# Eight heads at once: wide softmax stages, logarithm-and-Newton inverse lengths and two-bank evacuations in a two-attention kernel

## The chip, the cores and the metric

One core of one Trainium2 chip runs the kernel; all arithmetic is fp32 (two masks are bf16). The metric is the device time of one execution in microseconds. Before the change three runs gave 1178.49 to 1179.34 us, median 1179.04 us.

## The reference, cut to what matters

Eight sequences of 512 rows and 128 features go through a first attention (16 query heads on 8 key heads, causal, full length), a residual and a layer norm. Then come two layers of a windowed attention with a gated feed-forward, and a last layer norm.

```python
def _layer(x, wqkv, qs, ksc, wo, lg, lb, w1, b1, w2, b2):   # twice
    q, k, v = split(shift_token(x) @ wqkv)     # 8 heads of 64
    q = l2norm(q) * qs; k = l2norm(k) * ksc    # each head to length 1
    q, k = rotary_xpos(q, k)
    o = local_attention(q, k, v)               # windows of 64 see themselves and the one before,
    x = x + o @ wo                             # softmax over 128 keys, scores times 8
    h = (layer norm of shift_token(x)) * lg + lb
    a, g = split(h @ w1 + b1); h = a * gelu(g)
    return x + h @ w2 + b2
```

## The kernel before

The rows are cut into 32 tiles of 128. The first attention (steps whose names begin with a_) goes tile by tile through 8 batches of 4 tiles; a tile's keys grow from 128 to 512. The second attention (b_ steps) handles one tile of one layer at a time; such a pair is called a place here, and there are 64. A layer-1 place follows its layer-0 place by a group or two of two tiles, and the last two tiles are groups of their own. The feed-forward runs by groups.

**Order.** No queue is left to chance. `make_plan` lists every step with its engine, a cost in ns, the steps it needs, and the PSUM banks that it fills and who empties them. `in_order` simulates the five engines from these costs, the handover times `LAG` and `MARGIN` and the priorities `HURRY`, and writes out a fixed order for each engine and a bank for each PE step. Every engine then walks its list and waits on semaphore counts. PE's steps have a shape of the array (`HALF`, `TURN`, `COLS`, `QUARTER`); a change of shape has a price in the plan. Where PE has a planned gap over `IDLE` it gets `warm` fillers, products of the identity that nobody reads.

**One place of the second attention.** PE turns the tile (`b_h`, two banks), ACT and DVE copy it out, and PE makes q, k and v (`b_q`, `b_k`, `b_v`). ACT squares q and k (L901, L907). DVE multiplies them with two rotary tables (L1062, L1065) and POOL adds the halves (L1249). DVE sums the squares by head, for q (L1113, L1115) and k (L1120, L1122) apart, each with a floor; POOL raises both to the power -0.5 (L1262 for q, L1266 for k) and scales k (L1272). q stays unscaled. PE transposes q and k by halves of the partitions into two banks (L758); ACT copies out one bank (L922) and DVE the other (L1095). PE makes the scores of 8 heads in two banks (L776). DVE, for one head at a time, multiplies the scores with q's inverse length (keys carry a minus sign), adds the mask, writes to `b_prob` and keeps the minimum (L1107, eight a place). ACT, one head at a time, takes the exponential with that as bias and adds up the row (L930, eight a place). DVE takes the reciprocal (L1127), and POOL (L1279; ACT, L939, in the last three places) scales the probabilities. PE transposes them into two banks (L791), which ACT (L946) and DVE (L1133) copy out; then come the products with v (L807, copied to `o_t` by ACT, L952) and `wo`, a DMA shift by one row, the layer norm and the feed-forward (gelu L970, gate L1168 on DVE).

`b_prob`, `rnorm` and `r1` are two deep, PSUM has 8 banks. ACT's exponential and gelu lie in different table sets, and the loads (ACT_TABLE_LOAD) are put in by the compiler. All matrix steps of one bank go through the helper at L623 or lines of their own.

## Time and profile before

| what | before |
|---|---|
| median of 3 runs | 1179.04 us (1178.49 to 1179.34) |
| span of the profiled execution | 1177.7 us |
| what lies around that span, against the median | 1.4 us |
| busy: PE, DVE, ACT, POOL | 1151.3, 1047.6, 1010.3, 958.5 us |
| weight loads of PE | 827.0 us |
| granted TensorE clock, mean | 1.000 |
| instructions | 45569 |

The span runs from the first to the last instruction on the core. No time of the profiled execution other than its span is given. Busy time of an engine is the time in which at least one of its instructions ran; a busy PE can still be a PE whose matmuls wait for one another. PEld is the loading of weights, which goes on beside the matmuls. The shares are means over the whole kernel, whose middle repeats batch by batch and whose end has no first attention left to run.

### The profile page before, as it was taken

What the parts mean: (1) busy time and instruction counts of PE and PEld (TensorE: products, weight loads), DVE (VectorE), ACT (ScalarE), POOL (GpSimd) and SP (SyncE); (2) the same over time, 40 slices, a digit from 0 to 9 for tenths busy, and PEclk for the clock granted to TensorE, in tenths of its full rate; (3) what the DMA queues carried; (4) which work ended last, traced back from release to release, by engine and by line L of the source; (5) the groups of instructions that cost most, each with busy time, mean ns of one, the idle gap of its engine ahead of it and who ended that gap; (6) DMA issues with size and microseconds to landing.
All of it is one profiled execution on the core that took longest, in us unless ns stands there. A gap on an engine that the chain in (4) does not pass through costs nothing.

```text
span 1177.7 us, 45569 instructions
## 1 busy us (share of the span) xinstructions
PE 1151.3 (98%) x17652; PEld 827.0 (70%) x17652; DVE 1047.6 (89%) x4019; ACT 1010.3 (86%) x3168; POOL 958.5 (81%) x950
## 2 busy tenths in 40 slices
PE   9999999999999999999999999999999999999997
PEld 7667766767667667677676776777766767666666
DVE  6888998989999999989989899898998989999883
ACT  6888889897988989899898988889799887987784
POOL 2777878889878897888888888888987889888772
PEclk9999999999999999999999999999999999999999
DMA  6000010100011010100100101001101100010110
GB/s 228 19 13 22 16 30 22 27 14 22 21 27 27 14 31 12 31 23 22 31 17 18 27 19 31 16 18 28 26 13 26 27 13 23 12 31 19 24 27 13
DMA packets 31095, 31.87 MB, mean 27 GB/s; under 512 B 12576, under 2 KB 21408, under 8 KB 30752
## 3 DMA queue, kind: packets, MB, share of 16 engines
q1 hardware_dynamic: 30448, 28.17, 9.2%
q8 instruction: 141, 2.31, 0.8%
q10 hardware_dynamic: 432, 0.79, 0.2%
q14 instruction: 74, 0.61, 0.2%
HBM read 10.07 MB, written 2.10 MB: 10 GB/s over the span
## 4 chain that ended last, share of the span: by engine, by line
PE 78%; ACT 12%; DVE 5%; issue 2%; POOL 1%; DMA 1%; SPq 0%; POOLq 0%; DVEq 0%; ACTq 0%
PE psum L623 36%; PE psum L662 11%; PE psum L698 11%; PE psum L675 6%; PE psum L776 5%; PE psum L807 4%; ACT b_prob L930 3%; PE psum L791 3%; PE psum L758 2%; ACT prob L874 2%; ACT L930 2%; ACT L970 1%; ACT u_t L970 1%; ACT b_prob_t L946 1%; DVE x L1190 1%
## 5 line engine op out<-in xcount | busy, mean ns | idle before, releaser
L874 ACT ACTIVATE prob<-prob,negmax 128x512 f32<-128x512 f32 (+3 forms) x512 | 283.4, 558 | 9.6 <-DVE negmax L1025 9.2
L1025 DVE CUSTOM_DVE_ANT_0 prob<-psum,causal 128x512 f32<-128x512 f32 (+3 forms) x512 | 228.3, 484 | 7.0 <-PE psum L662 6.5
L1229 POOL TENSOR_SCALAR prob<-prob,rowinv 128x384 f32<-128x384 f32 (+1 forms) x256 | 161.2, 644 | 58.9 <-DVE rowinv L1031 58.4
L930 ACT ACTIVATE b_prob<-b_prob,b_negmax 128x128 f32<-128x128 f32 x512 | 198.9, 394 | 0.5 <-DVE b_negmax L1107 0.2
L623 PE MATMUL psum<-wqkv,h_t 128*64 128x512 f32 x768 | 191.5, 595 | 0.7 <-ACT h_t L894 0.5
L662 PE MATMUL psum<-k_t,q_t 64*128 64x384 f32 (+3 forms) x1024 | 179.5, 452 | 5.7 <-ACT b_prob_t L946 1.8
L1249 POOL TENSOR_TENSOR r<-r 128x512 f32<-128x512 f32 x120 | 152.7, 1277 | 10.8 <-DVE r L1065 10.5
L698 PE MATMUL psum<-prob_t,v 128*64 128x256 f32 x1280 | 152.3, 379 | 0.1
L1107 DVE CUSTOM_DVE_ANT_0 b_prob<-psum,band,rnorm 128x128 f32<-128x128 f32 x512 | 146.0, 347 | 6.9 <-PE psum L776 5.6
L1279 POOL TENSOR_TENSOR b_prob<-b_prob,b_rowinv 128x1024 f32<-128x1024 f32 x61 | 116.2, 1905 | 39.3 <-DVE b_rowinv L1127 39.3
L698 PEld LDWEIGHTS psum<-prob_t,v 128*64 128x64 f32 x1280 | 91.4, 137 | 59.0 <-issue 23.7
L1037 DVE COPY prob_t<-psum 128x512 f32<-128x512 f32 (+1 forms) x176 | 112.2, 638 | 7.4 <-PE psum L675 4.4
L675 PEld LDWEIGHTS psum<-ident,prob 64*128 64x128 f32 x2560 | 98.3, 139 | 26.2 <-issue 21.6
L1266 POOL TENSOR_TENSOR rnorm<-length,minus_half 128x8 f32<-128x8 f32 x64 | 106.0, 1656 | 9.4 <-DVE length L1122 9.3
L1232 POOL TENSOR_TENSOR prob<-prob,rowinv 128x512 f32<-128x512 f32 x96 | 99.2, 1053 | 15.9 <-DVE rowinv L1031 15.9
L675 PE MATMUL psum<-ident,prob 64*128 64x64 f32 x2560 | 111.1, 224 | 1.0 <-ACT b_prob_t L946 0.2
L1262 POOL TENSOR_TENSOR rnorm<-length,minus_half 128x8 f32<-128x8 f32 x64 | 106.3, 1661 | 4.5 <-DVE length L1115 4.5
L881 ACT COPY prob_t<-psum 128x512 f32<-128x512 f32 (+1 forms) x176 | 96.4, 548 | 13.5 <-PE psum L675 12.0
L874 ACT ACTIVATION_READ_ACCUMULATOR prob<-prob,negmax 128x1 f32 x512 | 98.8, 193 | 0.0
L930 ACT ACTIVATION_READ_ACCUMULATOR b_prob<-b_prob,b_negmax 128x1 f32 x512 | 98.3, 192 | 0.0
L623 PE MATMUL psum<-f_t,w 128*64 128x256 f32 (+1 forms) x816 | 91.4, 370 | 0.4 <-ACT f_t L961 0.3
L1062 DVE TENSOR_TENSOR r<-psum,table 128x512 f32<-128x512 f32 x128 | 86.6, 677 | 2.5 <-PE psum L623 1.1
(104 smaller groups left out, 2739.8 us busy)
## 6 DMA issues: line engine op xcount, KB each, us to landing
vb_mid<-vb SPq DMA_DIRECT2D x112, 128.0 KB, 2.3
x_t<-in_x_t SPq DMA_DIRECT2D x8, 256.0 KB, 3.1
x_n<-in_x SPq DMA_DIRECT2D x8, 256.0 KB, 2.9
x<-x SPq DMA_DIRECT2D x64, 31.8 KB
out<-x SPq DMA_DIRECT2D x15, 128.0 KB, 2.3
wqkv<-in_wqkv SPq DMA_DIRECT2D x1, 1536.0 KB, 11.3
w<-in_w SPq DMA_DIRECT2D x1, 768.0 KB, 13.4
x<-x SPq DMA_DIRECT2D x48, 0.2 KB
```

The costliest lines, as they stand in the source:

```text
L623: last = mm(out[half(w)], weights[:, half(w)], moving, start=start, stop=stop)
L662: last = mm(banks[h][:, p * K:(p + 1) * K], q_t[half(h), (NT * b + i) % 2, c + p, :], k_t[half(h), b % 2, (c + p) // 2, 0:K], start=True, ...
L675: last = transpose(banks[q][:, o:o + E], prob[half(q), k % PROBS, h, j * P:(j + 1) * P], ident[half(q), half(q)])
L698: last = mm(bank[half(h), p * P:(p + 2) * P], v[:, (NT * b + j) % V_RING, g * E:(g + 1) * E], two_pairs(k % PROB_TS, np_, i, h, p, j), sta ...
L874: last = af(pr, pr, ACT.Exp, bias=negmax[:, k % 4, o:o + 1], scale=-1.0, accum_out=rowsum[:, k % 4, o:o + 1])
L930: last = af(pr, pr, ACT.Exp, bias=b_negmax[:, a, o:o + 1], scale=-1.0, accum_out=b_rowsum[:, a, o:o + 1])
L1025: vec.tensor_tensor_reduce(prob[:, k % PROBS, h, p * K:(p + 1) * K], bank[:, p * K:(p + 1) * K], causal[:, S - K:S], -E ** -0.5, 3.0e38, A ...
L1037: vec.tensor_copy(prob_t[:, k % PROB_TS, 1, 0:n], bank[:, 0:n]).then_inc(prob_t_dve, 1)
L1107: vec.tensor_tensor_reduce(b_prob[:, a, s, c, :], bank[:, c * P:(c + 1) * P], band[:, min(n % NT, 2 - n % 2), :], rnorm[:, a, 0, 2 * c + s ...
L1229: last = gp.tensor_scalar(pr, pr, rowinv[:, k % 4, h:h + 1], 1.0, ALU.mult, ALU.mult)
L1249: return gp.tensor_tensor(r1[:, a, s, :, :], r1[:, a, s, :, :], r2[:, s, :, :], ALU.add)
L1279: gp.tensor_tensor(pr, pr, b_rowinv[:, a, :].unsqueeze(2).broadcast_to([P, HB, P]), ALU.mult).then_inc(b_prob_ready, 1)
```

## The change

The diff rewrites the second attention's side work and leaves PE's matmuls as they are.

- **Softmax in one operation a stage.** DVE adds the mask to the scores of all 8 heads out of both banks (`b_mask`), and takes the maxima of all heads in one reduction (`b_max`). POOL subtracts them (new step `b_less`). ACT takes one exponential over 1024 columns, with no bias and no accumulator. DVE adds up the rows in one reduction ahead of the reciprocal (`b_inverse`).
- **Inverse lengths.** DVE reduces the squares of q and k together and floors them (`b_length`). ACT makes a first guess as exp(-0.5 ln(65536 length)) (`b_guess`), DVE improves it by one Newton step of three small operations (`b_root`), and POOL scales both q and k (`b_unit`) before the transposition. The two powers on POOL go. The rotary table carries the factor LIFT, and the minus sign of the keys goes.
- **Evacuations over two banks.** Where a step fills two banks (`BESIDE`), the planner now gives it neighbours. ACT alone copies out the transposed q/k and probabilities, 1024 columns at once, save in the last 8 places (`SPLIT`), where ACT and DVE still share them. The copies of h and of the normed tile take both banks in one instruction.
- **Tables.** One set that holds exponential and logarithm is used for all exponentials, and the loads are written out.
- **The plan.** Costs, `HURRY` and two constants of `in_order` are new, so the orders of all engines are, too.

```diff
+LIFT = 65536.0
+TABLE_OF = {"exp": "natural_log_exp_and_others", "gelu": "gelu_and_others"}
 BANKS, LATE = 8, 15
-SINGLES, BY_ACT, BY_DVE = 2, 3, 8
+SINGLES, BY_ACT, BY_DVE, SPLIT = 2, 3, 8, 8
...
+def takers_of(l, n):
+
+    return ("act", "dve") if PLACE.get((l, n), -1) >= len(SEQUENCE) - SPLIT else ("act",)
+def wide_ns(taker, l, n):
+    return copy_ns(taker, 512) if len(takers_of(l, n)) == 2 else copy_ns(taker, 1024)
...
+SWITCH, TABLES, SHY, PULL = {"64x128": 155, "128x64": 150, "64x64": 97}, 1283, 381, 0.041587
+HURRY = {("act", "a_exp"): -50, ("act", "a_k"): 27100, ("act", "a_q"): 750, ("act", "a_turn"): 69350,
...
+BESIDE = ("b_h", "b_turn_qk", "b_scores", "b_turn_p", "b_turn_f")
...
+        step("dve", "b_length", k, 1400, [("act", "b_square_q", k), ("act", "b_square_k", k), before and ("dve", "b_root", before)])
+        step("act", "b_guess", k, 520, [("dve", "b_length", k), before and ("dve", "b_root", before)], "exp")
+        step("dve", "b_root", k, 750, [("act", "b_guess", k), before_2 and ("pool", "b_unit", before_2)])
...
+        step("pool", "b_unit", k, 1950, [("dve", "b_root", k), ("pool", "b_rotated_k", k), (summer(*k), "b_rotated_q", k)])
...
+        step("pe", "b_scores", k, 937, [(taker, "b_turn_qk", k) for taker in takers_of(l, n)], QUARTER, [[("dve", "b_mask", k)]] * 2)
+        step("dve", "b_mask", k, 1220, [("pe", "b_scores", k), ("dve", "tables", (LAYERS - 1,)), before_2 and ("pe", "b_turn_p", before_2)])
+        step("dve", "b_max", k, 1210, [("dve", "b_mask", k)])
+        step("pool", "b_less", k, 1900, [("dve", "b_max", k)])
+        step("act", "b_exp", k, 1040, [("pool", "b_less", k)], "exp")
+        step("dve", "b_inverse", k, 1400, [("act", "b_exp", k)])
+        step(scaler(*k), "b_scale", k, 1900 if scaler(*k) == "pool" else 3100, [("dve", "b_inverse", k)])
...
+                    if s.name in BESIDE:
+                        start = max(start, min(max(bank_free[x], bank_free[x + 1]) for x in range(0, BANKS, 2)))
+                    elif s.frees:
...
+            if s.name in BESIDE:
+                _, one = min((max(bank_free[x], bank_free[x + 1]), x) for x in range(0, BANKS, 2))
+                banks = [one, one + 1]
+            else:
+                clear = [x for x in range(BANKS) if bank_free[x] <= start]
+                banks = sorted(clear, key=lambda x: ((x ^ 1) in clear, bank_free[x], x))[:len(s.frees)]
...
+        def both_banks(name, *args):
+
+            one, two = BANK_OF[name, args]
+            return psum[:, one:two + 1, :]
...
+            nc.scalar.preload_act_table_set(TABLE_OF["exp"])
+
+            def table(name):
+
+                if function[0] != name:
+                    nc.scalar.preload_act_table_set(TABLE_OF[name])
+                    function[0] = name
...
+                rows = h_t[0:E, l, t * P:(t + 1) * P].rearrange("p (q n) -> p q n", q=2)
+                copy(rows, both_banks("b_h", l, n)[0:E, :, 0:E]).then_inc(h_act, 1)
...
+            def guess_lengths(l, n):
+                act.wait_ge(length_ready, nth("dve", "b_length", (l, n)))
+                act.wait_ge(rnorm_ready, nth("dve", "b_root", before(l, n)))
+                table("exp")
+                af(guess[:], length[:], ACT.Ln, scale=LIFT).then_inc(logged, 1)
+                act.wait_ge(logged, nth("act", "b_guess", (l, n)))
+                af(guess[:], guess[:], ACT.Exp, scale=-0.5).then_inc(guess_ready, 1)
...
+                if len(takers_of(l, n)) == 2:
+                    bank, _ = banks_of("b_turn_qk", l, n)
+                    copy(qk_t[:, l, :, :, k0:k0 + E].rearrange("p s c n -> p (s c) n"), bank.rearrange("p (k n) -> p k n", k=2 * CB)).then_inc(qk_act, 1)
+                else:
+                    act.wait_ge(cleared, 1)
+                    rows = qk_t[:, l, :, :, k0:k0 + P].rearrange("p s c (q n) -> p q (s c) n", q=2)
+                    copy(rows, both_banks("b_turn_qk", l, n).rearrange("p q (k n) -> p q k n", k=2 * CB)).then_inc(qk_act, 1)
+
+            def exponentials_b(l, n):
                 a = PLACE[l, n] % 2
-                for c in range(CB):
-                    act.wait_ge(b_max_ready, CB * (nth("dve", "b_max", (l, n, s)) - 1) + c + 1)
-                    pr = b_prob[:, a, s, c, :]
-                    o = s * CB + c
-                    last = af(pr, pr, ACT.Exp, bias=b_negmax[:, a, o:o + 1], scale=-1.0, accum_out=b_rowsum[:, a, o:o + 1])
-                last.then_inc(b_exp_done, 1)
+                act.wait_ge(b_less_ready, nth("pool", "b_less", (l, n)))
+                table("exp")
+                pr = b_prob[:, a, :, :, :].rearrange("p s c n -> p (s c n)")
+                af(pr, pr, ACT.Exp).then_inc(b_exp_done, 1)
...
-            def maxima_b(l, n, s):
+            def mask_b(l, n):
                 a = PLACE[l, n] % 2
                 dve.wait_ge(late_in, 16 * 7)
                 dve.wait_ge(tables_ready, LAYERS)
                 dve.wait_ge(b_scored, nth("pe", "b_scores", (l, n)))
                 dve.wait_ge(p_turned, nth("pe", "b_turn_p", before(l, n, 2)))
-                dve.wait_ge(rnorm_q, nth("pool", "b_inverse_q", (l, n)))
-                bank = banks_of("b_scores", l, n)[s]
-                for c in range(CB):
-                    o = s * CB + c
-                    vec.tensor_tensor_reduce(b_prob[:, a, s, c, :], bank[:, c * P:(c + 1) * P], band[:, min(n % NT, 2 - n % 2), :],
-                                             rnorm[:, a, 0, 2 * c + s:2 * c + s + 1], 3.0e38, ALU.add, ALU.min, b_negmax[:, a, o:o + 1]).then_inc(b_max_ready, 1)
-
-            def length_of_q(l, n):
...
-                dve.wait_ge(rnorm_q, nth("pool", "b_inverse_q", before(l, n)))
-                vec.tensor_reduce(ssq[:, 0, :, 0], sq[:, 0, :, :], AX.X, ALU.add).then_inc(summed_q, 1)
-                dve.wait_ge(summed_q, nth("dve", "b_length_q", (l, n)))
-                vec.tensor_reduce(length[:, 0, :], ssq[:, 0, :, :], AX.X, ALU.max).then_inc(length_q, 1)
-
-            def length_of_k(l, n):
                 dve.wait_ge(sq_k, nth("act", "b_square_k", (l, n)))
-                dve.wait_ge(rnorm_k, nth("pool", "b_inverse_k", before(l, n)))
-                vec.tensor_reduce(ssq[:, 1, :, 0], sq[:, 1, :, :], AX.X, ALU.add).then_inc(summed_k, 1)
-                dve.wait_ge(summed_k, nth("dve", "b_length_k", (l, n)))
-                vec.tensor_reduce(length[:, 1, :], ssq[:, 1, :, :], AX.X, ALU.max).then_inc(length_k, 1)
+                vec.tensor_reduce(ssq[:], sq[:], AX.X, ALU.add).then_inc(summed, 1)
+                dve.wait_ge(summed, nth("dve", "b_length", (l, n)))
+                vec.tensor_scalar(length[:], ssq[:], FLOOR, None, ALU.max).then_inc(length_ready, 1)
+
+            def roots(l, n):
+                a = PLACE[l, n] % 2
+                dve.wait_ge(guess_ready, nth("act", "b_guess", (l, n)))
+                dve.wait_ge(unit_ready, nth("pool", "b_unit", before(l, n, 2)))
+                link(vec.scalar_tensor_tensor(out=shortfall[:, 0], in0=guess[:], scalar=-0.5 * LIFT, in1=guess[:], op0=ALU.mult, op1=ALU.mult))
+                link(vec.tensor_tensor(shortfall[:, 1], length[:], shortfall[:, 0], ALU.mult))
+                vec.scalar_tensor_tensor(out=rnorm[:, a], in0=shortfall[:, 1], scalar=1.5, in1=guess[:], op0=ALU.add, op1=ALU.mult).then_inc(rnorm_ready, 1)
 
             def inverse_b(l, n):
                 a = PLACE[l, n] % 2
-                dve.wait_ge(b_exp_done, nth("act", "b_exp", (l, n, 1)))
+                dve.wait_ge(b_exp_done, nth("act", "b_exp", (l, n)))
+                vec.tensor_reduce(b_rowsum[:, a, :], b_prob[:, a, :, :, :].rearrange("p s c n -> p (s c) n"), AX.X, ALU.add).then_inc(b_summed, 1)
...
-            def inverse_length_of_q(l, n):
-                pool.wait_ge(length_q, nth("dve", "b_length_q", (l, n)))
-                pool.wait_ge(b_exp_done, nth("act", "b_exp", (*before(l, n, 2), 1)))
-                gp.tensor_tensor(rnorm[:, PLACE[l, n] % 2, 0, :], length[:, 0, :], minus_half[:], ALU.pow).then_inc(rnorm_q, 1)
-
-            def inverse_length_of_k(l, n):
-                pool.wait_ge(length_k, nth("dve", "b_length_k", (l, n)))
-                gp.tensor_tensor(rnorm[:, PLACE[l, n] % 2, 1, :], length[:, 1, :], minus_half[:], ALU.pow).then_inc(rnorm_k, 1)
-
-            def unit_k(l, n):
+            def unit(l, n):
                 a = PLACE[l, n] % 2
-                pool.wait_ge(rnorm_k, nth("pool", "b_inverse_k", (l, n)))
+                pool.wait_ge(rnorm_ready, nth("dve", "b_root", (l, n)))
                 pool.wait_ge(rotated_k, nth("pool", "b_rotated_k", (l, n)))
-                gp.tensor_tensor(r1[:, a, 1, :, :], r1[:, a, 1, :, :], rnorm[:, a, 1, :].unsqueeze(2).broadcast_to([P, HB, E]),
-                                 ALU.mult).then_inc(unit_ready, 1)
+                if summer(l, n) == "pool":
+                    pool.wait_ge(rotated_q, nth("pool", "b_rotated_q", (l, n)))
+                else:
+                    pool.wait_ge(rotated_q_dve, nth("dve", "b_rotated_q", (l, n)))
+                x = r1[:, a, :, :, :].rearrange("p s h e -> p (s h) e")
+                scale = rnorm[:, a, :, :].rearrange("p s h -> p (s h)").unsqueeze(2).broadcast_to([P, 2 * HB, E])
+                gp.tensor_tensor(x, x, scale, ALU.mult).then_inc(unit_ready, 1)
+
+            def less_maximum(l, n):
+                a = PLACE[l, n] % 2
+                pool.wait_ge(b_max_ready, nth("dve", "b_max", (l, n)))
+                pr = b_prob[:, a, :, :, :].rearrange("p s c n -> p (s c) n")
+                gp.tensor_tensor(pr, pr, b_maximum[:, a, :].unsqueeze(2).broadcast_to([P, HB, P]), ALU.subtract).then_inc(b_less_ready, 1)
...
-    for s, f in enumerate((scale * np.float32(8.0), np.float32(-1.0) / scale)):
+    for s, f in enumerate((scale * np.float32(8.0 * LIFT ** 0.5), np.float32(LIFT ** 0.5) / scale)):
...
```

## Rows read from the trace of the kernel before

**Rows 1.** Page, section 1: busy us, share of the span, instructions.
```profile
PE 1151.3 (98%) x17652; PEld 827.0 (70%) x17652; DVE 1047.6 (89%) x4019; ACT 1010.3 (86%) x3168; POOL 958.5 (81%) x950
```

**Rows 2.** Chain of waits, whole span: start us, us, what, pieces.
```profile
507.67 5.22 PE psum L623 x84
...
648.94 5.23 PE psum L623 x84
```

**Rows 3.** Windows: length, busy us (instructions) by engine, clock, DMA share, GB/s.
```profile
470.60:611.90 141.30, 139.89 (x2166) 100.53 (x2164) 129.07 (x499) 125.19 (x393) 121.39 (x120) 1.00 0.09 23
...
1035.80:1117.00 81.20, 77.38 (x1236) 53.60 (x1234) 74.15 (x262) 62.87 (x185) 65.19 (x58) 1.00 0.10 24
1117.00:1131.00 14.00, 13.49 (x225) 10.05 (x220) 12.37 (x53) 13.77 (x47) 7.79 (x8) 1.00 0.05 13
1131.00:1143.00 12.00, 10.58 (x186) 7.68 (x184) 11.63 (x40) 9.78 (x36) 10.54 (x10) 1.00 0.20 48
1143.00:1157.00 14.00, 11.44 (x210) 9.26 (x212) 5.65 (x30) 12.74 (x44) 3.67 (x4) 1.00 0.03 6
1157.00:1177.70 20.70, 15.03 (x262) 12.84 (x256) 9.38 (x36) 5.10 (x13) 7.95 (x11) 0.99 0.06 17
```

**Rows 4.** Groups by line, PE: the fillers.
```profile
L623 PE MATMUL psum<-ident 128*64 128x128 f32 x284 | 19.1, 276 | 0.0
```

**Rows 5.** Waits of PE's weight loads: us in total, times, longest us.
```profile
PEld psum L623 <- ACT o_t L952: 9.5, 16, 0.7
PEld psum L776 <- ACT qk_t L922: 5.8, 8, 0.9
PEld psum L623 <- DVE u_t L1168: 4.2, 12, 0.7
```

**Rows 6.** Timeline, 1143 to 1157 us: start us, us, engine, line, op, operands.
```profile
1146.11 0.34 DVE L1107 CUSTOM_DVE_ANT_0 b_prob<-psum,band,rnorm 128x128 f32<-128x128 f32 x1
...
1146.37 0.35 DVE L1107 CUSTOM_DVE_ANT_0 b_prob<-psum,band,rnorm 128x128 f32<-128x128 f32 x1
...
1152.06 0.20 DVE L1127 RECIPROCAL b_rowinv<-b_rowsum 128x8 f32<-128x8 f32 x1 [3.10 <-ACT b_prob L930]
...
1154.18 2.43 ACT L939 ACTIVATE b_prob<-b_prob,b_rowinv 128x128 f32<-128x128 f32 x8
```

**Rows 7.** Groups by line: length sum (DVE), power and scalings (POOL).
```profile
L1279 POOL TENSOR_TENSOR b_prob<-b_prob,b_rowinv 128x1024 f32<-128x1024 f32 x61 | 116.2, 1905 | 39.3 <-DVE b_rowinv L1127 39.3
...
L1266 POOL TENSOR_TENSOR rnorm<-length,minus_half 128x8 f32<-128x8 f32 x64 | 106.0, 1656 | 9.4 <-DVE length L1122 9.3
...
L1272 POOL TENSOR_TENSOR r<-r,rnorm 128x512 f32<-128x512 f32 x64 | 67.2, 1050 | 2.7
...
L1120 DVE TENSOR_REDUCE ssq<-sq 128x8 f32<-128x512 f32 x64 | 43.6, 682 | 2.9 <-ACT sq L907 2.1
```

**Rows 8.** Groups by line: DVE tensor_tensor out of PSUM, two widths.
```profile
L1062 DVE TENSOR_TENSOR r<-psum,table 128x512 f32<-128x512 f32 x128 | 86.6, 677 | 2.5 <-PE psum L623 1.1 <-ACT sq L901 0.7
...
L1144 DVE TENSOR_TENSOR x<-psum,x 128x128 f32<-128x128 f32 x64 | 18.3, 286 | 4.4 <-PE psum L623 4.3
```

**Rows 9.** Groups by line: evacuations by DVE and ACT.
```profile
L1095 DVE COPY qk_t<-psum 128x512 f32<-128x512 f32 x64 | 43.8, 684 | 0.3 <-PE psum L758 0.2
...
L922 ACT COPY qk_t<-psum 128x512 f32<-128x512 f32 x64 | 37.3, 583 | 17.4 <-PE psum L758 17.3
...
L894 ACT COPY h_t<-psum 64x64 f32<-64x64 f32 x128 | 20.0, 207 | 7.0 <-PE psum L721 7.0
```

**Rows 10.** Chain of waits, 1085 us to the end: table load, then exponentials.
```profile
1117.97 1.28 ACT L930
1119.27 3.19 ACT b_prob L930 x16
...
1123.26 1.54 ACT b_prob L930 x8
```

154 lines of the change are left out of this document (74 added, 80 removed), and 6 rows, old and new, of the table HURRY.

## Prediction

> **What bounds the kernel now.** I read the page's busy shares first. TensorE (PE) has 1151.3 of 1177.7 us, VectorE (DVE) 1047.6, ScalarE (ACT) 1010.3 and GpSimd (POOL) 958.5 [rows 1]. PE is the bound by share, but three others are close behind, so I then asked where PE isn't busy, and who ended that. The chain of waits shows that the middle of the kernel repeats: its 5.2 us projection piece comes back every 141.3 us, four times between 366 and 796 us, of which two rows stand there (507.67 and 648.94 us) [rows 2]. That is one batch: 4 tiles of the first attention and 8 places (tile and layer) of the second. The windows of that length (five from 188.0 to 894.5 us agree to 1 us, one stands there) say that of 141.30 us PE is busy 139.9, DVE 129.1, ACT 125.2 and POOL 121.4 [rows 3]. So in the middle PE idles 1.4 us a batch, some 10 us over the seven batches that look like this. The end is another stage: from 1035.8 us on PE idles 3.8 + 0.5 + 1.4 + 2.6 + 5.7 = 14.0 us [rows 3], and most of the 19.1 us of identity products into no result (fillers that keep PE going) [rows 4] lie there, too. About 30 us at the end is thus latency, not PE work. The clock is 1.00 throughout [rows 3], so clock plays no part.
>
> PE's own waits name mostly ACT as the releaser: its o_t 9.5 and its qk_t 5.8 us of weight-load idle, against 4.2 us for u_t, the largest of DVE's [rows 5]. An ACT queue that is served late is what PE sees most.
>
> **The change, part by part, per place (64 places).** PE's matmuls are the same in number and kind, so nothing is taken from or added to its work. What changes is how loaded the other engines are, how long the chain is, and PE's order, which the planner makes anew.
>
> *DVE.* Removed: eight masked maxima at a pitch of 0.26 us [rows 6], 2.08 us; two length reductions of 0.68 [rows 7] with a small floor operation each, which I put at the reciprocal's 0.2 [rows 6], 1.76 us. The reciprocal itself stays. Added: a masked copy of 1024 columns out of PSUM. A tensor_tensor from PSUM takes 286 ns for 128 columns and 677 for 512 [rows 8], 1.02 ns a column, so 1.20 us for 1024. A reduction of 512 columns takes 0.68, so one of 1024 about 1.20 by the same slope; there are three (maximum, row sum, squares), 3.60 us. The floor and three 16-column operations of the Newton step at 0.2 each, 0.8. Five waits of DVE on its own results, no row of their own, at about 0.05 each, 0.25. Added 5.85, removed 3.84: +2.0 us a place, +128 us in all. Back come the evacuations that ACT takes over whole in 56 of 64 places: 112 x 0.684 [rows 9] = -77 us, and one instead of two small copies of h, some -10 us at the reciprocal's 0.2. Net +41 us: DVE goes from 1047.6 to about 1089 us, and in a batch from 129.1 to 134.2 of 141.3 (95%). Bounds from the rows: +30 (no own waits, Newton operations at 0.15) to +60 (masked copy at the maxima's 0.26 us per 128 columns, 2.08, and no gain at h).
>
> *ACT.* Removed: eight exponentials, 3.19 with their accumulator reads [rows 10] (0.40 each). Added: one of 1024 columns without accumulation. A copy of 64 columns takes 207 ns, one of 512 583 [rows 9], 0.84 ns a column, so 1.01 us. Two 16-column functions (logarithm, exponential) at 0.2 to 0.3 each, 0.5. Two evacuations of 1024 columns in place of 512, +0.43 each in 7 of 8 places, 0.75. Net -0.93 us a place at face value; I take -0.86, for what of the two small functions is waiting, -55 us in all: 1010 to about 955.
>
> *POOL.* Removed: the two powers, 1.66 each, and the scaling of k, 1.050 [rows 7]. Added: scaling of q and k and the subtraction of the maximum, both 128x1024 with a broadcast as the probabilities' scaling has it, 1.905 each [rows 7]. Net -0.56 us a place, -36 us: 958 to about 923.
>
> *Table loads.* The logarithm now wants its set, which is made the one for all exponentials, so a load is still needed only between gelu and an exponential. A load shows as 1.28 us, and on the chain of the end the next function starts 1.30 us after the load began [rows 10]. The new logarithm can fall into a stretch of gelus and cost two loads more; if one place in eight does, 16 loads, 21 us of ACT, which its 55 us cover. The Trainium skill (ScalarE: Activation LUTs, What ACT_TABLE_LOAD costs) gives 1283 ns plus a drain of about 1380 ns for each switch. By that page's 2.66 us the same 16 loads would be an estimated 43 us, and ACT's relief would be all but gone. The trace shows the 1283 ns but not the drain, and I stay with the row.
>
> *The chain of one place* grows. Softmax, from scores to probabilities ready to be scaled: before 0.26 + 3.19 + 0.2 = 3.7 us if nothing interferes (ACT follows DVE head by head), after 1.20 + 1.20 + 1.91 + 1.01 + 1.40 plus five handovers of 0.1 = 7.2 us: +3.5. Lengths: before, k's reduction and floor 0.9, power 1.66 and scaling 1.05 (q's power is beside it), 3.6 us; after 1.37 + 0.5 + 0.6 + 1.91 + 0.4 = 4.8: +1.2, and it must wait for q's squares too. In the middle this is covered: the next places' work and the first attention's fill PE, each place of a layer has a period of 17.7 us, and the buffers are two deep. There the price is zero unless an engine saturates. If the cover fails, it is 4.7 us for each place in series.
>
> *PSUM banks.* Scores' second bank is now released after 1.2 instead of 2.1 us, both banks of a transposition after 1.0 instead of 0.6 to 0.7, and the two must be neighbours. These about cancel; zero, between -3 and +5 us.
>
> **The sum.** Middle: PE idles 1.4 us a batch, and the queue that mostly ends those waits loses 6.9 us a batch. I take 1.0 us of the 1.4 away: 7 x -1.0 = -7 us (bounds: -10, all of it, and +15, below). Start: nothing.
>
> End: three stages of the chain [rows 10]. From 1117 to 1131 it lies on ACT, 13.77 of 14.00 us busy [rows 3], and 6.3 us of it are exponentials of two places (3.19 and 1.54 [rows 10], and two more pieces of the same line, 1.6 together), which become 2.0: -4. From 1131 to 1143 it lies on DVE, 11.63 of 12.00 busy [rows 3], which gets one to two places' worth of +2.0: +3. From 1143 on one last place is alone: its softmax runs from 1146.11 to 1152.26 [rows 6], 6.15 us, and would take 7.2, but ACT's gelu and table load held its scaling back to 1154.18 anyway [rows 6]: 0. The last length step is 1 to 3 us longer: +2. Sum +1 us (bounds -6 and +10). What is late next there is DVE.
>
> Forecast: -7 + 1 = -6 us. The profiled span is 1177.7 us and the median of the three runs 1179.04, so 1.4 us lie around the span; I keep them. 1179.0 - 6 = 1173.0 us.
>
> The skill's page Trainium Kernel Development and Optimization (Performance Expectations) says that matmul busy time tells little of how near the bound PE is, and that the weight loads' busy share tells more. Here they differ, 98% against 70% [rows 1], so more than 1.4 us a batch may be hidden in PE's busy share. By that rule a new order could give more than my -7, and it is the reason for a lower end below the sum's.
>
> **Rivals.** *DVE takes PE's place.* At 134.2 of 141.3 us DVE has 7.1 us left a batch, where it has 12.2 now. Its order is fixed ahead, so a late operand idles it. For: it would be as full as the fullest engine, and every place needs it five times in series. Against: DVE waits little for others now (its largest waits are off PE's path), and PE's waits name ACT rather than DVE [rows 5]. It decides when DVE needs more than 7 us of idle a batch. If it needs 9 of today's 12.2, a batch is 134.2 + 9 = 143.2, +1.9 us, times 8 = +15, with the end's +1: 1195; if it needs 8, +0.9 a batch: 1187. About 1190. Chance 0.25.
>
> *The longer chain sets the end.* Two places (layer 0's last tile, then layer 1's) follow in series there. If ACT's relief doesn't come on that path, each pays up to 4.7: +8 to +9, and with no gain in the middle 1188, with the middle's gain 1181. Chance 0.12.
>
> *Nothing moves.* PE's 139.9 busy us a batch remain, and the 1.4 us aren't ACT's doing but shape changes and jitter. Then the middle gives 0, the end +-1, 1179. Chance 0.15.
>
> *The planner fills much better.* Forty microseconds less work on the three side engines together let it drop fillers and changes of PE's shape; all 10 us of the middle and 6 us of the end: 1163. I count it with the forecast. Chance of forecast and this together 0.48.
>
> **How the numbers follow.** One per mille is 1.2 us; about 0.2% (2.4 us) is what a measurement of this kernel can tell from no change. Faster by more (below 1176.7) is the forecast, 0.48. Within 0.2% is the third rival, 0.15, of which its jitter gives nothing away: 0.15. Slower (above 1181.4): 0.25 + 0.12 = 0.37. Both signs are likely, so the range goes over both: down to 1160, the forecast's best case with 3 us for the unseen, up to 1192, which takes most of the DVE rival. The forecast's own range is 1162 to 1176.
>
> **What the profile after would show.** Right: a period under 140.5 us, PE idle under 0.8 us a batch, ACT near 955, DVE near 1089, POOL near 923 us. DVE rival: DVE above 95% of the middle windows, PE waits that name DVE's b_prob, b_rowinv or rnorm, a period above 142. Chain rival: the middle as forecast, but more fillers and PE idle after 1035 us. Wrong outright would be table loads that take far more of ACT than 80 us, or DVE's new operations costing over 7 us a place.

## The result and the profile after

The change makes the kernel slower: 1292.37 us median of four runs (1288.91 to 1293.72) against 1179.18 us for the kernel before on the same chip, a ratio of 1.0958 with a 95% interval of 1.0942 to 1.0975. The profiled execution took 1293.54 us, its span is 1291.7 us, and the mean granted clock 0.992. I had forecast 1173.0 us and a range up to 1192.

Page of after, section 1 (busy us, share, instructions), against [rows 1]:

```profile
PE 1208.3 (94%) x17988; PEld 850.8 (66%) x17988; DVE 1134.3 (88%) x3074; ACT 944.8 (73%) x2236; POOL 929.9 (72%) x886
```

Groups by line of after, PE: the fillers, against [rows 4].

```profile
L657 PE MATMUL psum<-ident 128*64 128x128 f32 x620 | 40.5, 276 | 0.0
```

PE isn't busy for 1291.7 - 1208.3 = 83.4 us, where it was 26.4 before: 57 us. Its busy time grew by as much, though its real products are the same. The fillers take 21.4 us of that (40.5 against 19.1). The other 35.6 us lie in products that follow each other less closely, with more changes of shape (375 against 292, counted from the matmul records) and at a clock 0.8% lower; how much each of the three takes wasn't separated. No engine became the bound: the fullest is still PE, and DVE has 88% where it had 89%.

Windows of after, columns as in [rows 3], start, middle and end:

```profile
100.00:260.00 160.00, 150.21 (x2144) 103.13 (x2142) 142.06 (x407) 120.17 (x307) 119.68 (x114) 0.99 0.09 21
...
420.00:580.00 160.00, 147.80 (x2178) 101.35 (x2176) 142.93 (x381) 118.94 (x277) 119.80 (x113) 1.00 0.09 21
...
900.00:1060.00 160.00, 152.70 (x2320) 106.93 (x2317) 145.55 (x405) 126.54 (x297) 127.23 (x122) 1.00 0.08 20
...
1140.00:1220.00 80.00, 68.33 (x1104) 48.58 (x1100) 75.10 (x148) 41.41 (x79) 51.55 (x39) 1.00 0.07 18
1220.00:1291.70 71.70, 64.22 (x1098) 52.41 (x1094) 50.59 (x132) 38.62 (x83) 36.03 (x36) 0.98 0.07 19
```

The loss is spread over the whole kernel. In the middle PE idles 7 to 12 us of 160, where [rows 3] has 1.4 of 141.3; ACT and POOL idle 33 to 41 us each, and DVE 14 to 18. All four wait for each other. That is an order that doesn't fit, or a chain that isn't covered.

Waits of after (us in total, times, longest us), PE's weight loads, PE, and POOL:

```profile
PEld psum L822 <- POOL b_prob L1337: 25.2, 33, 1.7
PEld psum L807 <- ACT qk_t L975: 20.8, 33, 0.9
...
PE psum L696 <- DVE negmax L1078: 6.6, 12, 1.2
PE psum L822 <- POOL b_prob L1337: 6.2, 14, 0.8
```

```profile
POOL b_prob L1337 <- DVE b_rowinv L1183: 54.8, 38, 5.5
...
POOL r L1325 <- DVE rnorm L1176: 42.5, 45, 5.2
```

The weight loads now wait 25.2 us for the scaled probabilities and 20.8 for qk_t (5.8 in [rows 5]), and POOL, which delivers the first, waits for DVE's reciprocal and for DVE's Newton step.

Groups by line of after, the change's own steps (busy us, mean ns of one, idle before):

```profile
L1331 POOL TENSOR_TENSOR b_prob<-b_prob,b_maximum 128x1024 f32<-128x1024 f32 x64 | 122.1, 1908 | 43.5 <-DVE b_maximum L1161 43.5
L1325 POOL TENSOR_TENSOR r<-r,rnorm 128x1024 f32<-128x1024 f32 x64 | 122.0, 1907 | 51.8 <-DVE rnorm L1176 42.5 <-DVE r L1138 8.6
...
L1156 DVE TENSOR_TENSOR b_prob<-psum,band 128x1024 f32<-128x1024 f32 x64 | 77.9, 1218 | 4.2 <-PE psum L807 2.3 <-PE psum L822 1.4
L1166 DVE TENSOR_REDUCE ssq<-sq 128x16 f32<-128x1024 f32 x64 | 77.6, 1213 | 11.0 <-ACT sq L947 9.9 <-ACT sq L941 0.5
...
L894 ACT ACT_TABLE_LOAD x59 | 75.7, 1283 | 22.3 <-PE psum L657 21.6
...
L982 ACT ACTIVATE b_prob<-b_prob 128x1024 f32<-128x1024 f32 x64 | 67.5, 1056 | 4.8 <-POOL b_prob L1331 4.5
...
L1000 ACT COPY b_prob_t<-psum 128x1024 f32<-128x1024 f32 x56 | 56.7, 1013 | 49.2 <-PE psum L822 49.0
...
L1175 DVE TENSOR_TENSOR shortfall<-length,shortfall 128x16 f32<-128x16 f32 x64 | 31.8, 496 | 2.2
...
L1174 DVE SCALAR_TENSOR_TENSOR shortfall<-guess 128x16 f32<-128x16 f32 x64 | 29.1, 454 | 1.5 <-ACT guess L963 1.2
L1168 DVE TENSOR_SCALAR length<-ssq 128x16 f32<-128x16 f32 x64 | 28.9, 451 | 2.2
...
L1176 DVE SCALAR_TENSOR_TENSOR rnorm<-shortfall,guess 128x16 f32<-128x16 f32 x64 | 15.7, 245 | 2.2
```

Every large operation costs what the prediction said, within 5%: 1.22 us for the masked copy, 1.21 for a reduction, 1.06 for the exponential, 1.91 on POOL. The four small ones don't. They have 16 columns, and take 245 to 496 ns in the mean, 1.65 us a place where I had 0.8. Their spread says why. Instructions of one line, ns min/median/max:

```profile
L1168 DVE TENSOR_SCALAR length<-ssq x64: 174/232/1850, 48.6 to 1248.6; 128x16 f32<-128x16 f32 x64
...
L1174 DVE SCALAR_TENSOR_TENSOR shortfall<-guess x64: 134/176/1755, 55.6 to 1249.5; 128x16 f32<-128x16 f32 x64
...
L1175 DVE TENSOR_TENSOR shortfall<-length,shortfall x64: 174/176/1919, 56.2 to 1249.7; 128x16 f32<-128x16 f32 x64
...
L1183 DVE RECIPROCAL b_rowinv<-b_rowsum x64: 202/203/205, 83.7 to 1266.2; 128x8 f32<-128x8 f32 x64
```

The reciprocal takes 202 to 205 ns each of 64 times; the others take 0.17 us or anything up to 1.9, which is POOL's 1.9. The timeline of after at 689 us (start us, us, engine, line, op):

```profile
689.11 0.20 DVE L1183 RECIPROCAL b_rowinv<-b_rowsum 128x8 f32<-128x8 f32 x1
689.23 0.14 DVE L1174 SCALAR_TENSOR_TENSOR shortfall<-guess 128x16 f32<-128x16 f32 x1
689.39 1.90 POOL L1337 TENSOR_TENSOR b_prob<-b_prob,b_rowinv 128x1024 f32<-128x1024 f32 x1 [0.23 <-DVE b_rowinv L1183]
689.40 1.91 DVE L1175 TENSOR_TENSOR shortfall<-length,shortfall 128x16 f32<-128x16 f32 x1
...
691.35 0.17 DVE L1176 SCALAR_TENSOR_TENSOR rnorm<-shortfall,guess 128x16 f32<-128x16 f32 x1
```

DVE's reciprocal lets POOL start its scaling at 689.39. DVE's next small product starts 10 ns later and ends when POOL's instruction ends: 1.91 us for 16 columns, on the chain of waits of that stretch. Here the order puts the Newton step right behind the instruction that wakes POOL. Of the 64 instructions of L1175, those beside which no POOL instruction ran took 174 to 177 ns (34 of them), and the 30 others 861 in the mean; for L1168 it is 174 to 176 (17) and 551, for L1174 141 to 176 (23) and 619.

A start right behind POOL's is the costliest case, not the usual one. Of the 256 instructions of these four lines, 76 took over 300 ns, and 74 of the 76 ended 14 to 33 ns after a POOL instruction did. Only 8 of them had started within 30 ns of that instruction's start; the others began in its midst and stood until it ended. Beside POOL's powers of one or two columns (L1294, L1342), during which 19 of them began, none stood still.

### The profile page after: what moved, and what is told of

The parts are those of the page before. It is cut to its first block, busy times and chain, and to the rows that moved or that the text cites. A ratio compares the mean times of both kernels' runs of the same rounds, so it can differ in the third digit from the quotient of the medians.

```text
span 1291.7 us, 44015 instructions
## 1 busy us (share of the span) xinstructions
PE 1208.3 (94%) x17988; PEld 850.8 (66%) x17988; DVE 1134.3 (88%) x3074; ACT 944.8 (73%) x2236; POOL 929.9 (72%) x886
## 4 chain that ended last, share of the span: by engine, by line
PE 30%; DVE 14%; ACT 4%; issue 3%; POOL 2%; DMA 0%; POOLq 0%; DVEq 0%; ACTq 0%
PE psum L657 15%; PE psum L696 4%; PE psum L732 3%; PE psum L839 2%; PE psum L807 2%; DVE b_rowsum L1181 2%; DVE prob L1078 2%; DVE ssq L1166 1%; PE psum L709 1%; PE psum L822 1%; DVE r L1114 1%; POOL b_prob L1337 1%; DVE r L1117 1%; PE psum L788 1%; ACT prob L915 1%
## 5 line engine op out<-in xcount | busy, mean ns | idle before, releaser
L696 PE MATMUL psum<-k_t,q_t 64*128 64x384 f32 (+3 forms) x1024 | 183.5, 459 | 29.0 <-DVE negmax L1078 6.6
L1325 POOL TENSOR_TENSOR r<-r,rnorm 128x1024 f32<-128x1024 f32 x64 | 122.0, 1907 | 51.8 <-DVE rnorm L1176 42.5
L732 PE MATMUL psum<-prob_t,v 128*64 128x256 f32 x1280 | 155.4, 383 | 3.8 <-DVE prob_t L1090 3.6
L1331 POOL TENSOR_TENSOR b_prob<-b_prob,b_maximum 128x1024 f32<-128x1024 f32 x64 | 122.1, 1908 | 43.5 <-DVE b_maximum L1161 43.5
L696 PEld LDWEIGHTS psum<-k_t,q_t 64*128 64x128 f32 x1024 | 80.8, 190 | 39.3 <-issue 18.6
L929 ACT COPY z_t<-psum 128x256 f32<-128x256 f32 (+1 forms) x112 | 45.0, 402 | 68.1 <-PE psum L732 67.4
L1000 ACT COPY b_prob_t<-psum 128x1024 f32<-128x1024 f32 x56 | 56.7, 1013 | 49.2 <-PE psum L822 49.0
## 6 DMA issues: line engine op xcount, KB each, us to landing
w<-in_w SPq DMA_DIRECT2D x1, 768.0 KB, 13.5
```

The source lines that it names most:

```text
L696: last = mm(banks[h][:, p * K:(p + 1) * K], q_t[half(h), (NT * b + i) % 2, c + p, :], k_t[half(h), b % 2, (c + p) // 2, 0:K], start=True, ...
L732: last = mm(bank[half(h), p * P:(p + 2) * P], v[:, (NT * b + j) % V_RING, g * E:(g + 1) * E], two_pairs(k % PROB_TS, np_, i, h, p, j), sta ...
L1325: gp.tensor_tensor(x, x, scale, ALU.mult).then_inc(unit_ready, 1)
L1331: gp.tensor_tensor(pr, pr, b_maximum[:, a, :].unsqueeze(2).broadcast_to([P, HB, P]), ALU.subtract).then_inc(b_less_ready, 1)
```

## The experiments

Three theories were on the table. **O**: the order is to blame, since the priority table `HURRY` doesn't fit the changed steps. **D**: the new operations themselves, by their load on DVE and the longer chain. **L**, a part of D: the small DVE operations of the lengths, which stand still beside GpSimd. In the runs whose table was "searched", the table (with the two constants `SHY` and `PULL`) was found by random changes, kept or dropped by the end that `in_order` itself works out from the kernel's costs. Such a search finds a good table, not the best one, and runs 9 and 12 show that two of them for the same steps can lie 11 us apart on the chip.

**Run 1. The old operations with the new priorities.**

```diff
-SWITCH, TABLES, SHY, PULL = {...}, 1283, 380, 0.04162
-HURRY = {("act", "a_exp"): -50, ("act", "a_k"): 2250, ...
+SWITCH, TABLES, SHY, PULL = {...}, 1283, 381, 0.041587
+HURRY = {("act", "a_exp"): -50, ("act", "a_k"): 27100, ...
```

> The kernel before, all its operations and planned costs untouched, with only the changed kernel's priority table (HURRY, and the two constants SHY and PULL) in the planner. Theory O (order: the fixed order of before was fitted to its own steps, and the loss is mostly that fit): the same instructions as before, but 1255 to 1275 us, with PE gaps and fillers spread over the whole span. Theory D (VectorE's added work sets the time): DVE's busy time stays at 1048 us, so the time stays at 1179 to 1190 us.

Measured: 1240.34 us, ratio 1.0522 (1.0492 to 1.0553). Page, section 1, and two waits:

```profile
PE 1187.5 (96%) x17896; PEld 840.9 (68%) x17896; DVE 1047.4 (85%) x4019; ACT 1014.8 (82%) x3166; POOL 957.4 (77%) x950
```

```profile
PEld psum L793 <- POOL b_prob L1281: 22.2, 32, 1.3
...
PEld psum L625 <- ACT o_t L954: 15.0, 32, 0.9
```

Not one operation was changed, DVE, ACT and POOL work nearly as long as before, and 61.6 us are lost. Even the wait for POOL's `b_prob` that after shows (25.2 us) is there at 22.2 us. O's range lay 15 us too high, D's ended 50 us too low. So a table that doesn't fit can cost more than half of the 113 us by itself. But this table was made for other steps (it has no entry for the old kernel's `b_length_q`, `b_length_k`, `b_inverse_q` and `b_inverse_k`), so what it costs the changed kernel is not told here but by run 8.

**Runs 2 and 3. Both sets of operations with no priorities at all.**

```diff
-HURRY = {("act", "a_exp"): -50, ...
+HURRY = {}
```

> The kernel before with an empty priority table; operations and costs untouched. Theory O: 1235 to 1255 us, since the order then follows the planner's plain rule. Theory D: 1179 to 1190 us.

> The changed kernel with an empty priority table. Together with p2 it gives the price of the operations alone, both orders being unfitted. Theory O: the changed kernel's table is worth little, so 1290 to 1310 us, and the distance to p2 is 40 to 60 us, about half of the measured 113. Theory D: the whole 113 us lie in the operations, so the distance to p2 is over 100 us.

Measured: 1249.88 us (1.0603) and 1334.26 us (1.1319, 1.1282 to 1.1356). Pages, section 1, in this order:

```profile
PE 1174.8 (94%) x17676; PEld 842.4 (68%) x17676; DVE 1061.6 (85%) x4019; ACT 1007.1 (81%) x3168; POOL 960.4 (77%) x950
```

```profile
PE 1210.7 (91%) x17932; PEld 861.2 (65%) x17932; DVE 1141.2 (86%) x3074; ACT 936.8 (70%) x2232; POOL 928.0 (70%) x886
```

For the old operations the new table is worth 9.5 us over none, and their own 71.1 us. For the new ones it is worth 41.9 us. With neither fitted the operations cost 84.4 us. That is more than the 40 to 60 that O allowed them and less than the 100 and more of D, so neither does alone.

**Run 4. One reciprocal for the Newton step, in after's order.**

```diff
-af(guess[:], guess[:], ACT.Exp, scale=-0.5).then_inc(guess_ready, 1)
+af(guess[:], guess[:], ACT.Exp, scale=0.5).then_inc(guess_ready, 1)
...
-link(vec.scalar_tensor_tensor(out=shortfall[:, 0], ...))
-link(vec.tensor_tensor(shortfall[:, 1], length[:], shortfall[:, 0], ALU.mult))
-vec.scalar_tensor_tensor(out=rnorm[:, a], ...).then_inc(rnorm_ready, 1)
+vec.reciprocal(rnorm[:, a], guess[:]).then_inc(rnorm_ready, 1)
```

> The changed kernel in its own order (planned costs untouched), but ScalarE makes exp(+0.5 ln) and VectorE takes one reciprocal, in place of the three operations of the Newton step, whose correction is left out. In the changed kernel's trace those three take up 72 us of VectorE's own time (up to 1.9 us for 16 columns while GpSimd runs), the reciprocal should take 0.2 us each, 13 us in all. Theory L (VectorE's operations with two SBUF operands stand still while GpSimd's run, and this time is on the path): DVE busy falls by 55 to 65 us and the time by 20 to 60 us. Theory O: DVE busy falls alike, the time by under 15 us, since the order stays.

Measured: 1258.49 us (1.0676), 33.9 us less than after, with PE, ACT and POOL walking the same instructions in the same order. Page, section 1; DVE had 1134.3:

```profile
PE 1196.2 (95%) x17988; PEld 844.3 (67%) x17988; DVE 1074.9 (86%) x2946; ACT 942.5 (75%) x2236; POOL 927.2 (74%) x886
```

(Newton's correction of the guess is left out in this run and in runs 5, 6, 9, 11 and 12.)

**Run 5. Three reciprocals in a chain: as many instructions as the Newton step.**

```diff
-vec.reciprocal(rnorm[:, a], guess[:]).then_inc(rnorm_ready, 1)     # run 4's line
+link(vec.reciprocal(shortfall[:, 0], guess[:]))
+link(vec.reciprocal(shortfall[:, 1], shortfall[:, 0]))
+vec.reciprocal(rnorm[:, a], shortfall[:, 1]).then_inc(rnorm_ready, 1)
```

> As p4, in the changed kernel's own order, but VectorE takes three chained reciprocals (the reciprocal of the reciprocal of the reciprocal, 16 columns each) where the changed kernel has the three operations of the Newton step and p4 has one reciprocal. So the count of operations and of VectorE's waits on itself is the changed kernel's; what differs is that each reads one SBUF operand instead of two. Theory L (standing still beside GpSimd is the cost): each takes 0.2 to 0.25 us whatever GpSimd does, DVE busy is 25 to 30 us above p4's 1074.9, and the time is 1262 to 1272 us, near p4's 1258. Theory K (the count of small dependent operations in the chain is the cost): near the changed kernel's 1292 us.

Measured: 1265.62 us (1.0740). The second of the three, ns min/median/max:

```profile
L1175 DVE RECIPROCAL shortfall<-shortfall x64: 252/253/255, 56.4 to 1222.6; 128x16 f32<-128x16 f32 x64
```

Three instructions cost 7.1 us more than one; the Newton step's three cost 33.9. Alone, a reciprocal of 16 columns is slower than an operation of the Newton step (0.25 against 0.17 us). So 27 of the 34 us come from the standing still and not from the number of instructions: L holds, and K is refuted.

**Run 6. Run 4 with the floor as a reduction, too.** `ssq` gets a second column that holds the floor, and the larger of the pair is taken.

```diff
-vec.tensor_scalar(length[:], ssq[:], FLOOR, None, ALU.max)
+vec.tensor_reduce(length[:], ssq[:], AX.X, ALU.max)
```

> As p4, and the floor of the lengths is a reduction over pairs (as in the kernel before) instead of a tensor_scalar, which in p4 takes 0.17 us without GpSimd and 0.52 us on average beside it. Order untouched. Theory L: the reduction takes 0.17 to 0.2 us always, DVE busy falls by 13 to 20 us against p4 and the time by 5 to 15 us, to 1243 to 1254 us. Theory K: one operation in place of one, 1258 us as p4.

Measured: 1252.67 us (1.0630), 5.8 us less than run 4. Page, section 1:

```profile
PE 1195.6 (96%) x17988; PEld 844.4 (68%) x17988; DVE 1062.4 (85%) x2947; ACT 941.1 (75%) x2236; POOL 927.0 (74%) x886
```

In after's own order the four small operations thus cost 39.7 us more than the two that stand in for them, and what is left over run 1 (old operations with this table) is 12.3 us. PE's order and fillers are after's in runs 4 to 6, and yet PE is busy for 12.7 us less in run 6: matmuls that wait lengthen its busy time, too.

**Runs 7 to 9. Searched tables: the old operations, the new ones, and the new ones with the edits of run 6 in the order of run 8.**

```diff
-SWITCH, TABLES, SHY, PULL = {...}, 1283, 380, 0.04162           # run 7's lines
-HURRY = {("act", "a_exp"): -50, ...
+SWITCH, TABLES, SHY, PULL = {...}, 1283, 454.82248856686056, 0.08537289022901001
+HURRY = {("act", "a_exp"): 1450, ("act", "a_k"): 120450, ...
```

> The kernel before, operations and costs untouched, with a priority table found from an empty one by 600000 random trial changes that were kept or dropped by the planner's own simulated end (1180.5 us there, against 1195.1 for before's table and 1260.4 for none). Theory O: the table sets the time, so this is within 2% of before on either side, 1160 to 1200 us, and 50 to 90 us under the 1249.9 us of the empty table.

> The changed kernel, operations and costs untouched, with a table found in the same way (best of six searches: 1220.1 us in the planner, against 1302.5 for the changed kernel's own). Theory O: a good part of the measured 113 us comes back, 1205 to 1250 us, and what is left against q1 (40 to 50 us) is the price of the operations. Theory D (VectorE's load sets the time): DVE busy stays at 1134 us, so the time stays above 1270 us.

> q2 in its own order (costs untouched) with p6's two replacements: one reciprocal in place of the Newton step (its correction is left out) and the floor by a reduction. Theory L: DVE busy falls by some 75 us to about 1060, and the time falls by 20 to 40 us below q2, as p6 did below the changed kernel (40). Theory O alone: a better order hides it, under 10 us.

Measured: 1167.69 us (ratio 0.9912, 0.9897 to 0.9927), 1235.63 us (1.0485, 1.0467 to 1.0502) and 1183.19 us (1.0037, 1.0024 to 1.0050). Pages, section 1, in this order:

```profile
PE 1144.0 (98%) x17620; PEld 820.7 (70%) x17620; DVE 1043.6 (90%) x4019; ACT 1005.6 (86%) x3168; POOL 959.7 (82%) x950
```

```profile
PE 1183.6 (96%) x17944; PEld 850.9 (69%) x17944; DVE 1136.7 (92%) x3074; ACT 942.7 (76%) x2238; POOL 928.8 (75%) x886
```

```profile
PE 1168.4 (99%) x17944; PEld 841.5 (71%) x17944; DVE 1048.3 (89%) x2947; ACT 942.7 (80%) x2238; POOL 926.2 (78%) x886
```

A table that fits takes 56.7 us off the changed kernel, with no operation changed: this is what its own table cost it. It takes 11.1 us off the old one too: run 7 is the fastest kernel of all. The distance between runs 7 and 8 is 67.9 us, not the 40 to 50 expected. Between runs 8 and 9 PE's order, the fillers and everything on ACT and POOL are the same; four small operations are two others, DVE works 88.4 us less, and the time falls by 52.4 us, more than the 20 to 40 expected. PE's gaps between matmuls fall from 43.4 to 6.7 us. In run 8, 27 of the 40 us in gaps over 0.15 us ended with DVE, 16.5 of them with its copies of v, though DVE's mean share is only 92%:

```profile
PE psum L697 <- DVE v L1070: 9.3, 6, 1.6
PE psum L710 <- DVE v L1070: 7.2, 6, 1.9
```

Instructions of one line in run 9, the floor and the reciprocal, which now take nearly the same time each of 64 times:

```profile
L1170 DVE TENSOR_REDUCE length<-ssq x64: 185/186/188, 62.3 to 1136.6; 128x16 f32<-128x32 f32 x64
...
L1176 DVE RECIPROCAL rnorm<-guess x64: 210/245/253, 66.6 to 1137.5; 128x16 f32<-128x16 f32 x64
```

**Runs 10 to 12. What the other parts are worth, each with a table searched for it.** Run 10 is the kernel before with the wide copies; run 11 adds the lengths in the form of run 9; run 12 adds the wide softmax, which makes it the whole change, corrected.

```diff
+LEN, SOFT = 0, 0     # run 10;  2, 0 in run 11;  2, 1 in run 12
...
+step("dve", "b_root", k, 250 if LEN == 2 else 750, ...)
```

> One part of the change alone: before's softmax (per head) and before's inverse lengths (two powers on GpSimd), but the transposed q/k and probabilities are copied out by ScalarE alone, 1024 columns at once, save in the last 8 places, and the copies of h and of the normed tile take both banks in one instruction. The priority table was searched for these steps from an empty one, as for q1 and q2; the plan's own time is 1195.1 us (q1, with before's steps: 1180.5, before itself 1195.1). It tells whether the evacuations moved to ScalarE give back what the prediction credited to them: some 87 us less of DVE's busy time for some 48 us more of ScalarE's. Theory O (the order decides, and these moves relieve an engine that does not bound): DVE near 965 us, ScalarE near 1060, time 1168 to 1190, that is within 1% of before and not below q1's 1167.7. Rival R (relieving DVE alone is worth the 7 us and more that the prediction expected of it): under 1160. Rival S (ScalarE becomes the bound, since it now alone releases both banks of PE's transpositions): above 1195, with PE waiting for ScalarE's qk_t.

> Two parts of the change, in a corrected form: the wide copies as in r1, and the inverse lengths by one reduction of all squares, the floor as a reduction, logarithm and exponential (+0.5) on ScalarE, and one reciprocal on DVE (the Newton correction is left out); q and k scaled together on GpSimd. The softmax stays per head as before. Own searched table, plan's own time 1201.8 us. It has none of the small operations that stand still beside GpSimd, and GpSimd loses its two powers (212 us) for 55 us more of scaling. Theory L (the cost of the change's lengths is the small two-operand operations standing still): DVE near 970 us as in r1, GpSimd near 810 us, time 1172 to 1192, close to r1. If instead the longer lengths' chain itself (ScalarE in it, twice, and q's squares waited for) costs PE time, the time is over 1200 with PE waiting for GpSimd's r or for qk_t.

> The whole change with its lengths in the corrected form of r2 (reciprocal for the Newton step, which is left out, floor by reduction), and the plan told so: b_root costs 250 ns in the plan, not 750, and the priority table was searched anew for these costs; the plan's own time is 1205.9 us (q3 used the order of q2, planned 1220.1, and took 1183.2 us). Against r2 it adds only the softmax in one operation a stage. Theory O: a plan shorter by 14 us brings some of it on the chip: 1170 to 1183 us, at best level with before. Theory D (the wide softmax loads DVE beyond what PE leaves it): like q3 or above, 1183 to 1200, with DVE near 1048 us and 8 to 20 us slower than r2.

Measured: 1189.36 us (1.0092, 1.0077 to 1.0107), 1191.64 us (1.0112, 1.0095 to 1.0129) and 1194.43 us (1.0134, 1.0119 to 1.0149). Run 11 doesn't compute the reference's result. Where it departs wasn't found; my guess is the sign of the scores ahead of the minimum. Number, size and waits of its operations are as described, so its time is used as the cost of these operations and for nothing else. Pages, section 1:

```profile
PE 1156.7 (97%) x17768; PEld 831.4 (70%) x17768; DVE 974.0 (82%) x3843; ACT 1042.4 (88%) x3068; POOL 955.1 (80%) x950
```

```profile
PE 1173.0 (99%) x17764; PEld 824.8 (69%) x17764; DVE 956.3 (80%) x3779; ACT 1058.1 (89%) x3200; POOL 806.9 (68%) x822
```

```profile
PE 1175.3 (99%) x17860; PEld 831.7 (70%) x17860; DVE 1055.2 (88%) x2947; ACT 945.5 (79%) x2238; POOL 925.8 (78%) x886
```

Run 10 speaks against rival R (under 1160 us): 70 us less on DVE and 37 more on ACT bring nothing against run 7, but 21.7 us more. That no table for these steps would reach 1160 isn't shown. Of the 21.7, 8.2 us are one wait for an input at the start (first row below), behind which the granted clock is 0.76 for a stretch (second row, a window), an estimated 2 us more (8.2 x 0.24). In the other orders PE waits for an input for 0.8 us at most in the first 35 us, save run 11 (2.5 us, third row), whose clock stays at 1.00. Fillers, 26.1 against 16.5 us, are another 9.6. What is left is about 2 us.

```profile
PE psum L680 <- DMA x_t<-in_x_t: 8.2, 1, 8.2
```

```profile
22.50:30.70 8.20, 8.20 (x92) 7.37 (x94) 2.13 (x14) 4.57 (x18) 0.00 (x0) 0.76 0.01 2
```

```profile
PE psum L680 <- DMA x_t<-in_x_t: 2.5, 1, 2.5
```

The softmax in one operation a stage (run 12 against run 11) moves 99 us onto DVE, 119 onto POOL and 113 off ACT, and costs 2.8 us. The lengths (run 11 against run 10) take 148 us off POOL, and cost 2.3 us, or about 8 with the wait for the input (8.2 and 2.5 us) taken out of both. The expectation under D had 8 to 20 us for the softmax; the time itself lies in D's range (1183 to 1200), above O's. All these differences of a few us are smaller than what two searched tables can differ by, and tell no more than that neither part costs much. PE's busy time without fillers is 17.0 us longer in run 11 than in run 10 (1147.6 and 1130.6), and it changes shape 503 times instead of 316, which would be some 0.09 us a change. Run 12 fits that (483 changes, 1144.6 us), and so do runs 7 and 9 (340 and 360; 1127.5 and 1131.6). But run 8 has run 9's 360 changes and 1146.8 us, by its waits, so the changes are one likely cause and weren't tried alone. In run 12 the better costs gave a plan 14 us shorter than run 9's order and a kernel 11.2 us slower. A shorter plan is thus no sure gain. Of these spans seven lie 8 to 17 us below the plan's own end. Run 9, where DVE is faster than its planned costs, lies 39 below (runs 4 to 6 in after's plan 38 to 52), and run 1 lies 42 below, which I can't explain. Runs 3 and 8, which have the small operations, are 13 to 18 above (after has them too, and is below; why, stays open):

| kernel | the plan's own end, us | span measured, us | difference |
|---|---|---|---|
| before | 1195.1 | 1177.7 | -17.4 |
| after | 1302.5 | 1291.7 | -10.8 |
| run 1 | 1280.6 | 1238.5 | -42.1 |
| run 7 | 1180.5 | 1166.0 | -14.5 |
| run 2 | 1260.4 | 1247.9 | -12.5 |
| run 3 | 1312.2 | 1330.6 | +18.4 |
| run 8 | 1220.1 | 1232.9 | +12.8 |
| run 9 | 1220.1 | 1181.1 | -39.0 |
| run 10 | 1195.1 | 1187.5 | -7.6 |
| run 11 | 1201.8 | 1189.9 | -11.9 |
| run 12 | 1205.9 | 1192.4 | -13.5 |

## Why the prediction was wrong

**The account of the 113 us.** By one way (before, run 1, run 6, after): order 61.6, what is left of the operations 12.3, the four small operations 39.7; sum 113.6 us. By the other (before, run 7, run 9, run 8, after): a better order for the old operations -11.1, the rest of the operations 15.5, the small operations 52.4, the fit of the table 56.7; sum 113.5. So the order has 57 to 62 us, the small operations 40 to 52 us, and the rest, the large ones which the prediction spent most of its lines on, 12 to 16 us. The first way prices the order with the old steps and the second with the new ones; that they agree so closely may be luck, since two searched tables for the same steps lay 11 us apart. The 15.5 us between runs 7 and 9 are less than what run 9 has more in fillers (36.8 against 16.5 us).

**The step that failed first: "PE's order, which the planner makes anew".** I costed it at nothing or a gain ("the planner fills much better"), and none of my rivals had it as a loss. But the planner optimises nothing: it follows a table, and the table was in the diff, ACT's entry for `a_turn` going from 850 to 69350. It is the fit of that table to the steps that keeps PE 98% busy: without any table the old operations lose 71 us (run 2). My inference from a middle that idles 1.4 us a batch to a gain of 7 us or a loss of 15 took the fullness of the old order for a property of the work. It was a property of the table. Both kernels even hold the answer: the end that `in_order` works out is 1195.1 us before and 1302.5 after, 107 us later, and 1220.1 with run 8's table. Nothing in the prediction uses that number. And the busy share did hide more than the 1.4 us: run 7's table alone took 11.1 us off, with 4.7 us less of PE's products without fillers (1132.2 and 1127.5).

**The step that failed second: "three 16-column operations of the Newton step at 0.2 each", and the floor with them.** Alone they take 0.17; in place, 1.65 us a place together. I had priced all four by the reciprocal of [rows 6], which reads one operand and never stands still. The row that would have warned me was in the trace of before: L1190, a DVE sum of two operands in SBUF, whose row below gives ns min/median/max. I had looked at no row by its spread, only at means.

```profile
L1190 DVE TENSOR_TENSOR x<-x x17: 291/456/1266, 257.4 to 1173.1; 128x256 f32<-128x256 f32 x15, 128x128 f32<-128x128 f32 x2
```

The Trainium skill states the rule, on its page SBUF — State Buffer (Who interferes with whom): DVE and GpSimd share a pair of ports as an exclusive lock, taken on DVE's side by an operation with two SBUF inputs or a `tensor_scalar` in a two-port mode, not by a `tensor_reduce`, and whoever comes second waits for the whole instruction. The trace agrees for L1174, L1175 and L1176, which have two SBUF inputs, and for the reductions. L1168 stood still like them, but that it ran in such a mode isn't shown. Where the rule alone doesn't do is beside POOL's powers, which read SBUF too: none of the 19 instructions that began there stood still.

**DVE's sum, +41 us, measured +86.7.** I count each instruction from the end of the one before it, so that overlaps count once. The four small operations are +50 (101 us against 51). The removed ones gave 6 us less than I had (240 against 246). The large added ones and the waits cost 28 us less (295 against 323 us). The evacuations, the copies of h and everything unnamed gave 69 us, not 87; in it are 4.7 us that L1246, two SBUF operands again, stood still longer. The 0.05 us for each of DVE's waits on its own results had no row; after has idle time of 2.2 us before L1168, L1175, L1176 and L1183 each, 0.03 us a time. A slip without effect: 17.7 us is the period of the places of both layers together, and a layer's own is 35.3. The bound of +60 was too low by 27, because no end of it took a small operation's price from beside POOL.

**ACT and POOL were right**: 944.8 and 929.9 us, against 955 and 923. **Table loads**: 60 (59 at L894 and one at the start), where before has 62 (31, 21, 9 and 1 by line), not 16 more. It cost nothing and saved nothing. So neither sign for "wrong outright" came: the loads took 77 us, under 80, and DVE's new operations 6.2 us a place, under 7. No sign was set for the order. **The large operations' durations** were right within 1.5% (masked copy 1.22, reductions 1.21, scaling 1.91, exponential 1.06 against 1.01, 5%).

**The middle, -7 us.** Wrong in sign, and not for want of ACT's relief: PE's waits named ACT, ACT got 65 us lighter, and its qk_t wait rose from 5.8 to 20.8 us. The wide copy isn't the reason: run 8 has the same copies in another order and waits 3.8 us for them (row of run 8):

```profile
PEld psum L808 <- ACT qk_t L976: 3.8, 8, 0.5
```

A releaser's name says what came last in that order, not that the engine is too full. Run 10 points the same way from the other side: with DVE relieved by 70 us nothing was gained. PE's own products set the time in a well-fitted order, so relief of any side engine is worth only what PE idles.

**The rivals.** "DVE takes PE's place" asked for over 95% in the middle windows; after has 89 to 91%, and its weight loads wait 0.6 us in all for DVE's b_prob, so it isn't what happened there. In the fitted order of run 8 there is something of it, at 92%, with PE waiting for DVE's copies of v; its price was put at 15 us, and the four small operations cost 52 there. "The longer chain sets the end" is refuted: the loss is in the middle as well, and run 9 has the same long chain and loses 4.4 us against before. "Nothing moves" and "the planner fills much better" are refuted by the result.
